# Four unused words behind each block of 128 weights in a directional convolution's TensorE operands

## The reference

```
n = gn(x)                                   # 32 groups of 8 channels
h = gelu(depthwise3x3(n, dw))               # exact GELU
maps = einsum('bchw,oc->bohw', h, pw) + pb  # o = 8 * 256
out = x + sum_i maps[:, i] * (roll(n, direction_i) - n)
```

## Time and profile before

| what | us |
|---|---|
| median of 3 executions | 2278.92 |
| lowest, highest | 2213.62, 2280.05 |
| span of the profiled execution (first to last instruction) | 2255.6 |

### The profile page before, as it was taken

The page is one execution under the profiler, slowest core; times in us unless marked ns, Lnnn a source line. Parts: engine busy times, 40 slices in busy tenths (PEclk is TensorE's granted clock), DMA queues, the critical chain, the costliest instruction groups (busy, mean ns, idle before and its releaser), DMA issues.

```text
span 2255.6 us, 28700 instructions
## 1 busy us (share of the span) xinstructions
PE 2201.9 (98%) x10752; PEld 2014.8 (89%) x10752; DVE 2067.1 (92%) x2234; ACT 1842.6 (82%) x2762; POOL 1976.3 (88%) x857
## 2 busy tenths in 40 slices
PE   1999999999999999999999999999999999999998
PEld 1999999999999999999999999999999999999997
DVE  7999999999999999989999899999999999989895
ACT  5979888798888978888788887878878788787774
POOL 5889998999989988898888988889889998988985
PEclk9999999999999999999999999999999999999999
DMA  6245372543626444263443725337254372543424
GB/s 180 49 84 118 50 143 62 107 97 56 150 33 123 98 84 105 50 129 76 90 99 51 145 58 102 88 64 157 33 106 96 53 155 34 106 99 50 98 33 74
DMA packets 47083, 202.13 MB, mean 90 GB/s; under 512 B 3040, under 2 KB 7136, under 8 KB 45664
## 3 DMA queue, kind: packets, MB, share of 16 engines
q0 software_dynamic: 30192, 94.97, 26.1%
q1 hardware_dynamic: 16752, 105.34, 18.2%
HBM read 104.88 MB, written 146.80 MB: 112 GB/s over the span
## 4 chain that ended last, share of the span: by engine, by line
PE 92%; DVE 5%; ACT 1%; issue 1%; DMA 0%; POOL 0%; SPq 0%; DVEq 0%; ACTq 0%
PE psum L914 92%; DVE psum L775 2%; DVE products L702 1%; DVE psum L784 1%; DVE psum L702 0%; DMA acc<-x 0%; ACT psum L587 0%; ACT psum L555 0%; DVE acc L724 0%; ACT hid L569 0%; DVE acc L756 0%; POOL hlo L332 0%; DVE fields L807 0%; DVE part_sums L794 0%; DVE products L759 0%
## 5 line engine op out<-in xcount | busy, mean ns | idle before, releaser
L587 ACT ACTIVATE psum<-psum,bias,rstd 128x448 f32<-128x448 f32 x1792 | 1203.9, 694 | 368.6 <-PE psum L914 364.1
L914 PE MATMUL psum<-hhi,w_hi 128*128 128x448 f32 x3584 | 1312.7, 366 | 46.1 <-ACT hhi L574 45.4
L363 POOL TENSOR_TENSOR acc<-acc,products 128x896 f32<-128x896 f32 x333 | 1162.7, 3491 | 205.5 <-DVE products L702 197.6
L914 PE MATMUL psum<-hhi,w_lo 128*128 128x448 f32 x3584 | 1311.7, 366 | 0.0
L914 PE MATMUL psum<-hlo,w_hi 128*128 128x448 f32 x3584 | 1022.3, 366 | 0.3 <-POOL hlo L332 0.3
L784 DVE SCALAR_TENSOR_TENSOR psum<-xn,dw_f,psum 128x896 f32<-128x896 f32 x768 | 881.5, 1148 | 72.4 <-ACT psum L559 66.7
L914 PEld LDWEIGHTS psum<-hhi,w_hi 128*128 128x128 f32 x3584 | 671.9, 187 | 109.7 <-issue 45.4
L914 PEld LDWEIGHTS psum<-hlo,w_hi 128*128 128x128 f32 x3584 | 671.5, 187 | 62.2 <-POOL hlo L332 0.9
L914 PEld LDWEIGHTS psum<-hhi,w_lo 128*128 128x128 f32 x3584 | 672.0, 187 | 61.3
L702 DVE TENSOR_TENSOR products<-psum,fields 128x896 f32<-128x896 f32 x555 | 600.9, 1083 | 24.1 <-ACT psum L587 22.8
L702 DVE TENSOR_TENSOR acc<-psum,fields 128x896 f32<-128x896 f32 x224 | 241.6, 1086 | 45.8 <-ACT psum L587 45.3
(11 more groups left out here) (67 smaller groups left out, 448.2 us busy)
## 6 DMA issues: line engine op xcount, KB each, us to landing
out<-acc POOLq DMA_DIRECT2D x96, 896.0 KB, 7.7
out<-x SPq DMA_DIRECT2D x16, 3136.0 KB, 12.8
xpad<-x SPq DMA_DIRECT2D x30, 1568.0 KB, 14.8
out<-acc POOLq DMA_DIRECT2D x15, 448.0 KB, 5.6
acc<-x SPq DMA_DIRECT2D x4, 784.0 KB, 6.8
xpad<-pw_t SPq DMA_DIRECT2D x1, 2048.0 KB, 12.2
out<-products SPq DMA_DIRECT2D x2, 224.0 KB, 1.9
dw_f<-dw SPq DMA_DIRECT2D x1, 9.0 KB, 8.1
```

The source lines that it names most:

```text
L363: nc.gpsimd.tensor_tensor(a, a, p, ALU.add).then_inc(added_s, 1)
L587: nc.scalar.activation(m, m, ACT.Identity, bias=bias[ip][:, g, d:d + 1], scale=rstd[ip][:, g:g + 1]).then_inc(biased_s, 1)
L914: last = nc.tensor.matmul(maps(n0 * UNITS + q)[:, side, :], w[:, kk, col:col + P], h_part(h, t, nl, kk), start=s == 0, stop=s == len(steps ...
```

## The change

The tiles w_hi and w_lo get a third and a fourth dimension: for each input half, 16 blocks (BLOCKS) of 132 words (BLOCK_W), of which the first 128 are used. A block is now 528 bytes behind the one before, four times 128 and 16 over, so that block b of a half begins at (96 + 16 b) modulo 128, for both halves and both tiles (16 blocks are 66 times 128 bytes). Each tile grows by 512 bytes, and what lies behind them moves by 512 or 1024. The cast, the subtraction and the weight loads address the blocks' first 128 words. The order of instructions on each engine stays as it was.

```diff
--- before.py
+++ after.py
@@ -23,6 +23,7 @@
     STEPS = 2 * TILES
     BODIES = B // 2
     BANK = 512
+    BLOCKS, BLOCK_W = DIRS * C // P, P + 4
     SLICES = 2
     SROWS = H // SLICES
 
@@ -100,11 +101,12 @@
 
         first = sums_t[:, 0:HALVES * H * W]
         first = first.rearrange("p (g c r w) -> p g c r w", g=HALVES, c=SLICES, w=W)
+        w_blocks = xpad_t[1][:, 0:HALVES * DIRS * C].rearrange("p (k b m) -> p k b m", k=HALVES, m=P)
         w_raw = xpad_t[1][:, 0:HALVES * DIRS * C].rearrange("p (k m) -> p k m", k=HALVES)
 
         sb("gap", [P, 16])
-        w_hi = sb("w_hi", [P, HALVES, DIRS * C], F32R)
-        w_lo = sb("w_lo", [P, HALVES, DIRS * C], F32R)
+        w_hi = sb("w_hi", [P, HALVES, BLOCKS, BLOCK_W], F32R)
+        w_lo = sb("w_lo", [P, HALVES, BLOCKS, BLOCK_W], F32R)
         dw_f = sb("dw_f", [P, HALVES, 9])
         pb_f = sb("pb_f", [P, HALVES, DIRS])
         zeros = sb("zeros", [P, 2, WP])
@@ -401,7 +403,8 @@
             norm_scales(0, 0)
 
             pool.wait_ge(w_hi_s, 1)
-            nc.gpsimd.tensor_tensor(w_lo[:], w_raw, w_hi[:].bitcast(F32), ALU.subtract).then_inc(w_lo_s, 1)
+            nc.gpsimd.tensor_tensor(w_lo[:, :, :, 0:P], w_blocks, w_hi[:, :, :, 0:P].bitcast(F32),
+                                    ALU.subtract).then_inc(w_lo_s, 1)
 
             pool.wait_ge(first_s, FIRST)
             for axis in range(2):
@@ -831,7 +834,7 @@
             dve.wait_ge(weights_in, 16)
             join(w_raw, C, w_sum)
             dve.wait_ge(w_sum, PB_SUMS)
-            nc.vector.tensor_copy(w_hi[:], w_raw).then_inc(w_hi_s, 1)
+            nc.vector.tensor_copy(w_hi[:, :, :, 0:P], w_blocks).then_inc(w_hi_s, 1)
 
             dve.sem_inc(prod_s, PROD0)
             for c in range(3):
@@ -905,13 +908,13 @@
                     pe.wait_ge(hhi_s, n0 + need)
                 for side in range(2):
                     d, g = unit_map(u, side)
-                    col = d * C + g * P
+                    block_of = d * HALVES + g
                     steps = [(w, hhi, kk) for kk in range(HALVES) for w in (w_hi, w_lo)]
                     steps += [(w_hi, hlo, kk) for kk in range(HALVES)]
                     for s, (w, h, kk) in enumerate(steps):
                         if u == 0 and side == 0 and s == 2 * HALVES and wanted:
                             pe.wait_ge(hlo_s, n0 + need)
-                        last = nc.tensor.matmul(maps(n0 * UNITS + q)[:, side, :], w[:, kk, col:col + P], h_part(h, t, nl, kk),
+                        last = nc.tensor.matmul(maps(n0 * UNITS + q)[:, side, :], w[:, kk, block_of, 0:P], h_part(h, t, nl, kk),
                                                 start=s == 0, stop=s == len(steps) - 1)
                     last.then_inc(maps_s, 1)
```

## The result

| executions | kernel before, us | changed kernel, us |
|---|---|---|
| these, without a profile | 2213.62, 2280.05, 2278.92, 2213.50 | 2247.09, 2246.83, 2246.87, 2247.00 |
| median | 2246.27 | 2246.93 |

The changed kernel has one time, to within 0.26 us, and it lies halfway between the two of the kernel before. The ratio given for the pair is 1.0151 (95% interval 1.0133 to 1.0168); it is taken against the executions of the kernel before at its lower level alone, since those 3% above them count as disturbed, which here they are not: both levels are the kernel's own. So the change costs 1.5% against the best case of before and saves 1.5% against its worst. Against the median I had, 2278.92, it is 32 us less; I forecast 55 less, 2224.

What follows compares the result with a forecast made beforehand. It took 10,752 back-to-back matmuls on TensorE as the bound: 2212.9 us with all at 200.0 ns, plus 10,752 x 0.95 ns, gives 2223.1, plus about 1 us around the span: 2224 us. Range 2145 to 2300.

Steps and rivals of the forecast that it cites:

- The bound and the two levels: Back-to-back matmuls set the time, 200.0 or 206.7 ns apart, drawn at pauses and held: 2212.9 or 2278.3 us.
- The offsets matter: Weight loads beside running matmuls: the address relation of weights and streams may set the 13.3 and 20 ns over 186.7.
- the first rival: Offsets do nothing, both levels lie inside TensorE and are drawn at pauses: 2214 or 2279 us, likely 2279; chance 0.28.
- Step (3): Matmul distances: 896 disturbances each draw a level, six of seven 200.0, one 206.7; mean 200.95 ns, 10,752 x 0.95 ns added.
- Pauses at every image to the end: Sign of a right forecast: TensorE pauses for VectorE's product once an image throughout, ten more pauses, 3.9 us.
- Lower step: Rival: at some offsets reads miss one another, the matmul distance falls to 193.3 ns, 2142 to 2190 us; chance 0.14.
- slower rotation: Rival: the rotation passes through worse offsets, matmul distance up to 213.3 ns, 2351 us if in all; chance 0.24.
- Steps (4) to (6): Cast into w_hi (bounded by 3.2 us), subtraction into w_lo (up to 1.7 us), later tiles' move: each taken as 0.
- My reading of the addresses: Weight blocks begin at 96 modulo 128 bytes, moving operands at 0, so all 10,752 pairs meet in the same relation.
- step (2): Load-to-stream relation moves 16 bytes every 12 matmuls, shared by both sides of a unit; distance between 186.7 ns and 0.31 us.

Runs made afterwards that it cites:

- c64: Kernel before with a gap of 8 words for 16, every weight block at 64 modulo 128 instead of 96: median 2234.8 us.
- c0: Kernel before with a gap of 24 words, every weight block at 0 modulo 128 (128 modulo 256): median 2250.4 us.
- c32: Kernel before with a gap of 32 words, every weight block at 32 modulo 128: median 2264.8 us.
- h32: Kernel before with the streams hhi and hlo 32 bytes further on and the weights left at 96: 2234.9 us in both executions.
- kb64: Kernel before with one unit of eight's weight blocks at 64 modulo 256, the others at 96, cast and subtraction in five pieces: 2218.4 us.
- kbside: As kb64, but only the unit's second side (six matmuls, the last of the tile) at 64: 2217.5 us, 0.974 to the kernel before.
- w0: Kernel before with a gap of 56 words for 16, every weight block at 0 modulo 256: 2279.8 and 2270.3 us.
- kick64: Kernel before with one unit of eight's blocks at 64 modulo 128, later blocks moved by 128 bytes, not whole 256: 2245.3 us.
- lo16: Kernel before with all w_lo blocks 16 bytes further on (112 modulo 128) and w_hi left at 96: median 2255.8 us.

## Why the prediction was wrong

- **The bound and the two levels** held. The chain is the matmul line, each level holds to the next pause, and the executions of before fell at 2213 and 2280 again and again, as summed, or between them; beside c64 no execution of 23 was at 2213.
- **The offsets matter** held, and the first rival (they do nothing) is out: c64, c0 and c32 differ by 30 us by their gap alone. The rule of the Trainium skill, TensorE: Matmul & The Clock Gate (Part 2, what each phase is for), that loading the next weights takes nothing from the running matmul, doesn't make the offsets idle in this float32 case: by c64 and h32 the difference of the two operands' addresses sets the distance, though no row shows what the reads do. The 2.5 ns over the columns that the same page of the Trainium skill gives (Part 1, Wait — 56ns, not 53.3ns?) stand against 13.3 to 20.0 here.
- **Step (3) failed**, the draw. I took values from 200.0 and 206.7 only and let each unit draw one of them, six times in seven the lower. The term had the right sign (up from 200.0 ns) and the wrong size: 10,752 x 0.95 ns = 10.2 us, where the trace gives 203.64 - 200.0 = 3.64 ns, 39.1 us. Put into my own sum it closes: by the traces of kb64 and kbside an execution at the lower level pauses 15 times and not 16, so 2212.9 becomes 2212.5, and 2212.5 + 39.1 - 15 pauses of 0.39 us that go (5.9) = 2245.7, against a span of 2245.3. What was wrong under the number: distances are not drawn from two values. The two levels are what the placements 96 and 224 do when they are left alone; other placements have other patterns, and under moving blocks the changed kernel never holds a level (in its start times, at most three distances of 200 ns in a row, or five of 206 and 207). Nor do its four executions look like draws: they lie within 0.26 us. Disturbed and then left alone for 84 matmuls, 96 does go to the lower level (kb64), so the idea of my step was sound for a kernel with that rest between; in this change the rest is six matmuls, with a new offset each time (modulo 256 the two sides of a unit differ by 128).
- I wrote that the forecast fails if distances depend on the offset strongly, since I knew one of eight. It did, by that.
- **Pauses at every image to the end**: wrong. What is left is the one longer distance per image, some 35 ns over the mean, 0.5 us in all. In between the waits shrink: 15 of them, 6.7 us, in kb64 (means of 201.0 ns), 4.2 us in c64 (202.2), none in c0 (204.0).
- **Lower step and slower rotation**: neither. Single distances of 195 to 199 ns occur, but no offset tried has a mean under 200.0, nor over 206.7.
- **Steps (4) to (6)**, the cast, the subtraction, the tiles behind: cost 0, as taken.
- **My reading of the addresses** took modulo 128 from the change's own description. w0 against c0, and the breaks at each change of side in kick64, show that it is not the period, and the sides of a unit in the changed kernel (8 blocks apart, 128 modulo 256) are not in one relation, against what step (2) says.

Left open: what has the cycle of 6.67 ns; whether the extra time is reads that collide, which no row shows; whether 256 is the full period; why a disturbance at 64 leads back to the lower level and one at 112 not always; and a kernel with fewer weight loads, which was not tried.

## What to carry to other kernels

Where the matmul line is the chain, print the start-to-start distance over the whole span before anything else: one stable number, two that hold from pause to pause, or a short pattern tell what a busy share of 98% hides. Executions that fall into two groups on one core can be the kernel's own two patterns, not noise, and then a median says little; the placement of the stationary operand against the moving one alone moved this kernel between 2234.8 and 2279.8 us (2%), and 16 bytes on one tile (lo16) were enough to end the two levels. Spreading the placements over all offsets gave a steady time between the two levels; keeping the placement that has the lower one and disturbing it for six matmuls per tile, so that it returns to that level, bought 29 us more. Which disturbance does so has to be tried: 64 did in all 14 executions (kb64, kbside), 112 in three of eight.

## What was unexpected of the hardware

- The distance between matmuls depends on the difference of the operands' addresses, down to 16 bytes on one of two tiles (lo16), and with a period over 128 bytes: means for 448 columns are 202.2 ns (64), 204.0 (128 modulo 256), 205.3 (160), 206.7 (0, in its profile), and 200.0 or 206.7 (96 and 224).
- Under a constant placement the distances form cycles of 1, 3 or 5 matmuls whose sums are whole numbers of 6.67 ns (30 or 31, 91, 153 or 154), over thousands of matmuls; a pause or an odd distance once an image interrupts them, and they resume.
- One placement can have two such cycles; which one it is in is settled at a pause and then kept, 66 us of 2280.
- At 384 columns the lower pattern has the same 13.3 ns over the stream (173.3 ns) as at 448, so there it is a cost per matmul and not per column; the upper pattern has 16.7 for 20.0.
